# An int8 feed-forward stage as one straight block, its weights made one stage earlier, and layernorms whose channel halves are added on GpSimd

## What is computed

```python
def _layernorm(x, axis=-1, eps=1e-05):
    m = jnp.mean(x, axis=axis, keepdims=True)
    v = jnp.var(x, axis=axis, keepdims=True)
    return (x - m) / jnp.sqrt(v + eps)
def quant_act_uint8(x):                      # one scale for the whole tensor
    s = jnp.maximum(jnp.max(x), EPS) / 255.0
    return jnp.clip(jnp.round(x / s), 0.0, 255.0) * s, s
def quant_weight_int8_perchannel(w):         # one scale for each output channel
    s = jnp.maximum(jnp.max(jnp.abs(w), axis=1, keepdims=True), EPS) / 127.0
    return jnp.clip(jnp.round(w / s), -128.0, 127.0) * s, s[:, 0]
h = jax.nn.relu(quant_linear(x, w1, b1))     # w1: 1024 x 256
return quant_linear(h, w2, b2)               # w2: 256 x 1024; the bias is rounded to s_in * s_w
```

## Time and profile before

| | us |
|---|---|
| median of 3 runs | 4343.7 |
| lowest and highest of them | 4338.48, 4356.22 |
| the profiled execution | 4357.23 |
| its span in the trace | 4355.4 |
| TensorE busy in the span | 3932.3 (90%) |
| VectorE busy | 2478.7 (57%) |
| ScalarE busy | 1965.8 (45%) |
| GpSimd busy | 1533.3 (35%) |
| instructions | 69,479 |

### The profile page before, as it was taken

The page is one execution under the profiler, slowest core; times in us unless marked ns, Lnnn a source line. Parts: engine busy times, 40 slices in busy tenths (PEclk is TensorE's granted clock), DMA queues, the critical chain, the costliest instruction groups (busy, mean ns, idle before and its releaser), DMA issues. The chain is left out here.

```text
span 4355.4 us, 69479 instructions
## 1 busy us (share of the span) xinstructions
PE 3932.3 (90%) x26955; PEld 2098.6 (48%) x26967; DVE 2478.7 (57%) x3415; ACT 1965.8 (45%) x3546; POOL 1533.3 (35%) x1362
## 2 busy tenths in 40 slices
PE   6878965989999999999999999999999999998755
PEld 4443421645554555445554455435554455445423
DVE  3563454558842788238852688328862488424433
ACT  2454534446632466326643466326653366324311
POOL 0420000036630566116640466206651366300034
PEclk8998986899999999999999999999999999998877
DMA  4000000021120111101120111101111011100297
GB/s 145 1 1 22 0 20 10 1 85 29 29 69 0 34 28 27 60 16 30 28 74 0 29 28 31 61 12 29 28 32 47 24 28 29 47 0 11 83 284 190
DMA packets 95344, 185.48 MB, mean 43 GB/s; under 512 B 14004, under 2 KB 46256, under 8 KB 94000
## 3 DMA queue, kind: packets, MB, share of 16 engines
q1 hardware_dynamic: 86816, 169.02, 13.0%
q0 software_dynamic: 6144, 9.44, 1.2%
q10 hardware_dynamic: 2064, 2.62, 0.2%
HBM read 112.19 MB, written 20.09 MB: 30 GB/s over the span
## 5 line engine op out<-in xcount | busy, mean ns | idle before, releaser
L1569 PE MATMUL PS<-locw,X 128*128 128x512 f32 x2304 | 1066.0, 599 | 18.7 <-DVE locm L1773 10.1
L1836 POOL TENSOR_TENSOR locm<-locm 128x512 f32<-128x512 f32 x384 | 489.6, 1275 | 912.5 <-DVE locm L1773 912.1
L1569 PEld LDWEIGHTS PS<-locw,X 128*128 128x128 f32 x2304 | 394.8, 190 | 431.2 <-issue 299.4
L1954 PE MATMUL PS<-locxn,locw 128*128 128x512 f32 x960 | 423.8, 599 | 19.9 <-DVE loch L2072 19.9
L1842 POOL TENSOR_TENSOR locm<-locm,locrn 128x512 f32<-128x512 f32 x384 | 392.8, 1044 | 128.9 <-ACT locrn L1688 128.9
L1849 POOL TENSOR_TENSOR locpr<-locpr,locrs 128x512 f32<-128x512 f32 x384 | 391.5, 1041 | 128.8 <-DVE locrs L1802 108.9
L1771 DVE TENSOR_TENSOR locm<-PS,loctab 128x512 f32<-128x512 f32 x384 | 263.6, 687 | 211.3 <-ACT locsq L1678 211.3
L1709 ACT ACTIVATE locpt<-PS 128x512 f32<-128x512 f32 x384 | 208.4, 594 | 321.9 <-PE PS L1579 321.9
L2072 DVE SCALAR_TENSOR_TENSOR loch<-PS,locvec,locgl 128x512 f32<-128x512 f32 x144 | 106.8, 749 | 358.3 <-PE PS L1954 268.7
L1954 PEld LDWEIGHTS PS<-locxn,locw 128*128 128x128 f32 x960 | 181.6, 191 | 259.3 <-issue 229.4
L1713 ACT ACTIVATE locpr<-locpr 128x1024 f32<-128x1024 f32 x192 | 203.3, 1059 | 191.4 <-DVE locpr L1793 191.4
(11 more groups left out here) (322 smaller groups left out, 6323.5 us busy)
## 6 DMA issues: line engine op xcount, KB each, us to landing
locve<-locva SPq DMA_DIRECT2D x372, 128.0 KB, 2.2
locw<-in_L2f_wqkv SPq DMA_DIRECT2D x36, 512.0 KB, 9.4
BIG<-in_L3f_gu SPq DMA_DIRECT2D x16, 768.0 KB, 10.2
moe_sums<-none SPq DMA_DIRECT2D x2, 4352.0 KB, 23.9
locw<-in_L2f_w SPq DMA_DIRECT2D x6, 1386.0 KB
BIG<-moe_sums SPq DMA_DIRECT2D x16, 512.0 KB, 10.0
moewp<-in_L3f_gu SPq DMA_DIRECT2D x10, 768.0 KB, 16.8
loctab<-in_L2f_tabs SPq DMA_DIRECT2D x6, 1024.0 KB, 11.4
```

The costliest lines, as they stand in the source:

```text
L1569: mm = pe.matmul(PS[:, o % 2, :], k.X[:, j, at - j:at - j + P], W[:, j, col:col + G], start=j == 0, stop=j == KD - 1)
L1836: pool.tensor_tensor(M1[:, j, :], M1[:, j, :], M2[:, x, :], ALU.add).then_inc(s.paired, 1)
L1954: mm = pe.matmul(PS[:, 4 + 2 * (m % 2) + half, :], W1[:, c, at:at + P], XNL[:, g % 2, c, :], start=c == 0, stop=c == KD - 1)
```

## The change

- Layernorm. The loop is written out over four groups, in the order of the lists below. GpSimd adds the two channel halves of x, and of the squares, before the one matmul that makes the mean or the variance; a square takes both halves in one instruction; all four centred groups have room (XC). Hooks let a stage put work into each engine's list. The five separate layernorms all take this form. In the local transformer the wait for the saved residual moves from the front of VectorE's list to behind the second centre, and GpSimd's mask cast and table product go behind its sums.
- Weights. The int8 weights are loaded, measured and rounded in the slot stage, into parts of k.BIG that it leaves free: SP loads them behind the stage's own weights, VectorE measures at the end of units 0, 1 and 2, GpSimd rounds and clips ahead of its additions to X.
- The int8 stage. Its layernorm block also turns the weights (TensorE first, ScalarE copies), takes x's maximum group by group and reduces it. All that follows is one block without loops. x is scaled on ScalarE, clipped and raised on VectorE, lowered to bf16 on GpSimd. Of the 8 tiles of h ScalarE takes 6 and VectorE 2 (affine; their relu comes later, in raise_h). h is scaled by all three: 2 tiles with a plain copy and 2 with a relu on ScalarE, 4 on GpSimd. h's quantised groups, the outputs and the PSUM banks are double, and TensorE's waits are by halves of a group.
- The new helpers in words. raise_x(g): VectorE, min with 255, plus ROUND (128x1024). affine(g, m): VectorE, PSUM tile times scale plus bias. largest_h(g, half): maximum of tiles 0 to 2, or 3 to 7. fix(g): min with 255, plus ROUND on tiles 6 and 7. clip(g): two instructions of 4 tiles each, minus ROUND, min with 255, to bf16; the first waits for raised and the first lift, the second for fixed and the second lift. up(g) waits for lower_x(g) and for its PSUM tile to have been read. weigh(g): the two outputs with scale and bias.
- The stage has 27 semaphores of its own in place of 15; the slot stage has five more.

```diff
-def stage_layernorm(nc, k, src, shift=0, layer=0, affine=None, dest=None, beside=None):
+def stage_layernorm(nc, k, src, dest=None, beside=None):
...
+                    pool.tensor_tensor(XS[:, g % 2, :], x[:, 0, :], x[:, 1, :], ALU.add).then_inc(s.xs, 1)
...
+                    pool.wait_ge(s.sq, base + g + 1)
+                    sq = SQ[:, g % 2, :, :]
+                    pool.tensor_tensor(sq[:, 0, :], sq[:, 0, :], sq[:, 1, :], ALU.add).then_inc(s.ss, 1)
...
+                sum_x(0)
+                sum_x(1)
+                sum_squares(0)
+                sum_x(2)
+                sum_squares(1)
+                sum_x(3)
+                sum_squares(2)
+                sum_squares(3)
+                if beside:
+                    beside.pool_last(pool)
...
+                    pe.matmul(PS[:, g % 2, :], k.meanw[:, :], XS[:, g % 2, :], start=True, stop=True).then_inc(s.mean, 1)
...
+                if beside:
+                    beside.pe_first(pe)
+                mean(0)
+                mean(1)
+                variance(0)
+                mean(2)
+                variance(1)
+                mean(3)
+                variance(2)
+                variance(3)
...
+                centre(0)
+                centre(1)
                 if beside:
...
+                    beside.may_write(dve)
+                normalise(0)
+                centre(2)
+                normalise(1)
+                centre(3)
+                normalise(2)
+                normalise(3)
...
+                square(0)
+                square(1)
+                rstd(0)
+                square(2)
+                rstd(1)
+                square(3)
+                rstd(2)
+                rstd(3)
+                if beside:
+                    beside.act_last(act)
...
+def int8_weights(k, io):
...
+        pool.wait_ge(s.scaled, 1)
+        for m in range(FK):
+            link(pool.tensor_scalar(W1[:, m, :], W1[:, m, :], RW[:, m:m + 1], ROUND, ALU.mult, ALU.add))
+        for c in range(KD):
+            link(pool.tensor_scalar(W2[:, c, :], W2[:, c, :], RW[:, FK + c:FK + c + 1], ROUND, ALU.mult, ALU.add))
+        for w, q in ((W1, s.W1Q), (W2, s.W2Q)):
+            link(pool.tensor_scalar(w, w, ROUND, 127.0, ALU.subtract, ALU.min))
+            pool.tensor_scalar(q, w, -128.0, None, ALU.max).then_inc(s.quantised, 1)
...
+    ORDER = (0, 6, 1, 2, 7, 3, 4, 5)
+    AM = 6
...
+        def reduce_x(pool):
+            pool.wait_ge(s.x_max, 1)
+            pool.partition_all_reduce(MX[:, 0:1], S[:, 0:1], P, RMAX).then_inc(s.x_largest, 1)
...
+                def down(g):
+                    for half in range(2):
+                        pe.wait_ge(s.hq, 2 * g + half + 1)
+                        if g >= 2 and half == 0:
+                            pe.wait_ge(s.y, g - 1)
...
+                def raise_h(g):
+                    h = H[:, AM:FK, group(g)]
+                    act.activation(h, h, ACT.Relu, scale=R[:, 1:2]).then_inc(s.rectified, 1)
+                    h = H[:, 0:2, group(g)]
+                    act.activation(h, h, ACT.Copy, scale=R[:, 1:2], bias=ROUND).then_inc(s.raised, 1)
...
+                raise_h(0)
+                raise_h(1)
+                act.wait_ge(s.bias, 2)
+                weigh(0)
+                raise_h(2)
+                weigh(1)
+                raise_h(3)
+                weigh(2)
+                weigh(3)
...
+                def lower_x(g):
+                    pool.wait_ge(s.xu, g + 1)
+                    pool.tensor_scalar(XQ[:, :, group(g)], k.XN[:, :, group(g)], ROUND, None, ALU.subtract).then_inc(s.xq, 1)
...
+                for g in range(NG):
+                    lower_x(g)
+                pool.wait_ge(s.h_max, 1)
+                pool.partition_all_reduce(MX[:, 1:2], S[:, 1:2], P, RMAX).then_inc(s.h_largest, 1)
+                pool.wait_ge(s.h_scale, 1)
+                for g in range(NG):
+                    for m in (2, 4):
+                        h = H[:, m:m + 2, group(g)]
+                        pool.tensor_scalar(h, h, R[:, 1:2], ROUND, ALU.mult, ALU.add).then_inc(s.lifted, 1)
...
+                for g in range(NG):
+                    raise_x(g)
+                for g in range(NG):
+                    affine(g, 6)
+                    affine(g, 7)
+                    if g:
+                        largest_h(g - 1, 1)
+                    largest_h(g, 0)
+                largest_h(NG - 1, 1)
...
+                scale(1, s.h_scale)
+                bias(slice(FK, FK + KD), b2, 1)
+                fix(0)
+                clip(0)
+                fix(1)
+                clip(1)
+                add(0)
+                fix(2)
+                clip(2)
+                add(1)
+                fix(3)
+                clip(3)
+                add(2)
+                add(3)
...
+                    beside[1](dve, u)
...
+                beside[2](pool)
```

More of the change, by code:

```diff
@@ L143, in _, with mean @@
             @block.tensor
             def _(pe):
[L145 to L157, removed]
+                def mean(g):
+                    pe.wait_ge(s.xs, base + g + 1)
+                    if g >= 2:
+                        pe.wait_ge(s.xc, base + g - 1)
+                    pe.matmul(PS[:, g % 2, :], k.meanw[:, :], XS[:, g % 2, :], start=True, stop=True).then_inc(s.mean, 1)
@@ L159, in _, with centre @@
+                mean(3)
+                variance(2)
+                variance(3)
             @block.vector
             def _(dve):
-                if beside:
[L162 to L177, removed]
+                def centre(g):
+                    dve.wait_ge(s.mean, base + g + 1)
+                    for c in range(KD):
+                        op = dve.tensor_tensor(XC[:, g, c, :], cols(src, g)[:, c, :], PS[:, g % 2, :], ALU.subtract)
+                    op.then_inc(s.xc, 1)
@@ L179, in _ @@
+                normalise(0)
[4 more added lines that the diff above has]
+                normalise(3)
             @block.scalar
             def _(act):
-                nc.scalar.preload_act_table_set(LNEXP)
[L182 to L199, removed]
-                                xn = k.XN[:, c, bass.ds(b * L + h * G, G)]
-                                op = act.activation(xn, xn, ACT.Identity, scale=affine[0][:, c:c + 1], bias=affine[1][:, c:c + 1])
-                            op.then_inc(s.aff, 1)
@@ new lines, in fix, with clip @@
+                def fix(g):
+                    h = H[:, AM:FK, group(g)]
+                    dve.wait_ge(s.rectified, g + 1)
+                    dve.tensor_scalar(h, h, 255.0, ROUND, ALU.min, ALU.add).then_inc(s.fixed, 1)
+                def clip(g):
+                    for half in range(2):
+                        dve.wait_ge(s.lifted, 2 * g + half + 1)
+                        if half == 0:
+                            dve.wait_ge(s.raised, g + 1)
+                            if g >= 2:
+                                dve.wait_ge(s.y_ps, g - 1)
+                        else:
+                            dve.wait_ge(s.fixed, g + 1)
+                        ms = slice(4 * half, 4 * half + 4)
+                        dve.tensor_scalar(HQ[:, g % 2, ms, :], H[:, ms, group(g)], ROUND, 255.0, ALU.subtract, ALU.min).then_inc(s.hq, 1)
```

379 lines of the change are left out of this document (213 added, 166 removed).

## The result

| | before | changed |
|---|---|---|
| median of 6 runs, us | 4340.7 | 4320.8 |
| lowest and highest | 4335.0, 4356.2 | 4311.2, 4331.5 |
| ratio, 95% interval | | 0.9948 (0.993 to 0.9966) |
| the profiled execution, its span | 4357.2, 4355.4 | 4331.5, 4329.7 |

The kernel is faster by 20 to 23 us; 4316 was forecast, and the measured time lies inside the range. But the sum came out by terms that erred in opposite directions, and that is what the rest is about.

What follows compares the result with a forecast made beforehand. The int8 stage was taken as bounded by a chain, not an engine. Its -33.9 us, +0.9 for semaphores and +5.4 for layernorms gave -27.6, so 4316 us off the median 4343.7, range 4306 to 4328.

Steps and rivals of the forecast that it cites:

- The chain: Int8 stage, 141.9 us: engines take turns, so a chain bounds it and any step taken off is time saved.
- The layernorm: Five layernorm blocks: 25.9 us each with half the passes; sum of four +5.4 us (-1 to +7).
- Then the written order bites: Layernorm: list order makes a loop of centre, square, rstd and normalise, 5.2 us with handovers.
- The slot stage: Weights loaded, measured and quantised there fit into gaps and ahead of the additions to X: cost 0.
- if the slot stage grows by over 3 us: Sign that the forecast is wrong, beside absent or hidden switches or a down part over 40 us.
- half of a 7.1 us instruction: Slot stage: estimated leak of up to 3 us if VectorE's small tensor_scalar waits for GpSimd's port; taken as 0.
- rival B: Dearer port: VectorE's two-SBUF-input instructions also exclude GpSimd's; slot stage +8, down part +3, 4327 us; chance 0.20.
- The code switches: Int8 stage: four GpSimd code loads of 7 to 9 us around two reductions, the third hidden, the others exposed.
- rival A: Code loaded in time or TensorE stays at 2.4 GHz: 6 us at the first switches, 6 at T0; 4304, chance 0.17.
- The lowering's 1.15 us: Int8 stage: GpSimd lowers 1,024 columns of x in 1.15 us, ends 1.1 and 2.7.
- The down part: End of the int8 stage, from h's scale at T0 = 75.0: T0 + 33, between 30 undisturbed and 36 taking turns.
- The sum: Whole kernel: int8 stage -33.9, semaphores +0.9, layernorms +5.4, slot stage 0; net -27.6 us.

Runs made afterwards that it cites:

- e5: Changed kernel with both partition reductions of the int8 stage moved from GpSimd to TensorE and VectorE, without a code switch: 4311.7 us, 0.9916 of before.
- e6: Changed kernel with x raised by ScalarE and lowered on VectorE instead of GpSimd, upper clip left out: 4319.2 us, 0.9937 of before.
- e7: Changed kernel with the five layernorms' lists reordered (all sums, means, centres and squares first) and four buffers: 4285.8 us, 0.9871 of before.
- e4: Probe without the reference's sublayers: twenty blocks of GpSimd instructions beside VectorE ones; two SBUF inputs beside max lost 10.4 us against its 17.52.
- e1: Changed kernel with the int8 weights quantised on VectorE in its pauses instead of on GpSimd: 4314.5 us, 0.9927 of before.
- e10: The changed kernel again, unaltered, measured beside new runs of before: 4324.2 us, 0.9954 of before.
- e2: Changed kernel with each of GpSimd's two max instructions of the weights run twice: one run, 4335.4 us; first to last gate 227.1 us.

## Why the prediction was right, and where it was wrong

**The chain** as the bound of the int8 stage was right: e5 and e6 each took steps off it and shortened the stage by 7.8 and 6.6 us. That is what had been exposed of these steps, not their whole length: the two ways back of 6.9 and 6.7 us were in part covered by other engines' work.

**The layernorm**: "Then the written order bites" held, its size was too big. 25.9 us were forecast; 24.5 to 25.4 were measured, so +0.6 to +1.2 where +2.4 and +1.6 stood, and e7 shows that the order is more than all of it. In the local transformer -1.0 was forecast and nothing came: there GpSimd's table product met the last normalises, two of which took 4.0 us together for 1.29.

**The slot stage** is the step that failed, by the prediction's own sign ("if the slot stage grows by over 3 us"): "Cost 0. What could leak is VectorE's one small tensor_scalar per unit". It cost 10.9 us. Of these the tensor_scalar's wait of 6.9 us alone was more than the 3 us that I allowed for it, "half of a 7.1 us instruction"; I had halved a wait that can be whole. The rest is rival B: the instructions with two SBUF inputs do wait, as e4 shows by themselves and e1 by their wait going when GpSimd's work goes. I gave it 0.20 on the strength of one row that happened to begin where a max lets go. Its price there of 8 us was nearer than the 0 of the sum.

**The code switches** were right in their number and their place, except the first: 8.7 us were taken from a row of before (the weights' DMAs ran beside it; whether that made it longer no run shows), it took 6.3 at most, and VectorE's maximum came at the same moment, so the reduction ended at t = 31.4 where the sum had 35.3. That is a part of rival A. It put the first lowering at t = 38.7 for 43.1. The lowering's 1.15 us was wrong: 2.76, just beyond the upper end given. It cost the stage, since e6 gains 6.6 us without it and its switch, but TensorE still began at 41.6 for 44.3, and the maximum of h came at t = 69, not 74. Two of these 5 us are a slip of addition: 51.4, three groups of 5.95 and 2.8 make 72.0, not 74.0. Measured from group 0's first maximum at 48.3, the same terms give the 69.

**The down part**: T0 + 32.4 us for T0 + 33 (34.4 in e10). A lift took 2.1 us in the mean for 1.15; that VectorE and GpSimd take turns was in the sum.

**The sum**: from -27.6, the int8 stage -5.5, the slot stage +12.6, the layernorms and their neighbours -1.0 give -21.5. That the time came out well is luck: two errors of opposite sign met, and the range held both.

## What to carry over

Before moving work to GpSimd, list which of VectorE's instructions run beside it: those with an operand in PSUM and reductions are safe, tensor_scalars on SBUF wait out the whole GpSimd instruction, two SBUF inputs lost about 60% of the long ones here. A wait of that kind is priced by the longest GpSimd instruction that it can meet, so on a serial chain one small instruction can cost 7 us, and work that VectorE can do in its own pauses is better left there. And a hand-written order is a term of its own: the same layernorm took 25 or 16.5 us by nothing but the order of its lists and the buffers that this order needs.

## What was not expected

- GpSimd's price depends on the operation: per 1,024 columns, multiply-add 1.12 us, subtract to bf16 2.76, max to bf16 2.7 (5.36 for 2,048), subtract-min 3.5 (7.09). The same subtract-min of 2,048 columns took VectorE 1.22 us in e1.
- The stage behind the change follows the clock: the second cross attention took 142 to 153 us over these traces with the same instructions, 151.9 where its first 30 us ran at a granted 0.56 (the changed kernel), 143.1 where they ran at 0.84 (e5). It isn't the change that decides: in e10 the changed kernel itself had 0.85 and 143.0, and the kernel before 0.56 and 152.1. What does decide is not shown. Such differences are a part of the spread between single runs of one kernel, which is 16 to 20 us for the changed kernel and up to 33 for the kernel before.
- Doubling a suspected cost made it smaller (e2): the small tensor_scalar now met a shorter instruction.
